# Three-by-three maxima stored by the first stage and used by all classes, in a second stage whose neighbouring tiles are of different classes

## What is computed

```python
x = x + _L0_conv_ref(_gn(x), L0_conv_W, L0_conv_bias)   # 1x1 product over 512 channels + 25 descriptors
x = x + _L1_conv_ref(_gn(x), w1, b1, w2, b2)
# layer 1, for each of the 16 x 512 planes:
s = relu(score)                        # one number a plane, from the plane means through two small products
q_s = clip(floor(s), 0, 5); q_b = q_s + 1
pools = [x, max over 3x3, 5x5, 7x7, 9x9, 11x11, 13x13]       # stride 1, same size
return frac_b * pools[q_b] + frac_s * pools[q_s] + x
```

## Time and profile before

| | us |
|---|---|
| median of 3 runs | 4183.77 (4174.26 to 4189.22) |
| the profiled execution | 4180.08 |
| its span in the trace | 4177.9 |
| PE busy | 3474.2 (83%) |
| DVE busy | 3378.0 (81%) |
| POOL busy | 2087.4 (50%) |
| ACT busy | 1981.8 (47%) |

### The profile page before, as it was taken

The page is one execution under the profiler, slowest core; times in us unless marked ns, Lnnn a source line. Parts: engine busy times, 40 slices in busy tenths (PEclk is TensorE's granted clock), DMA queues, the critical chain, the costliest instruction groups (busy, mean ns, idle before and its releaser), DMA issues. The chain is left out here.

```text
span 4177.9 us, 72982 instructions
## 1 busy us (share of the span) xinstructions
PE 3474.2 (83%) x22600; PEld 1981.8 (47%) x22601; DVE 3378.0 (81%) x3619; ACT 1981.8 (47%) x3227; POOL 2087.4 (50%) x1576
## 2 busy tenths in 40 slices
PE   4999999999999999999999996567678666666554
PEld 3666666666665666666666664223233222222221
DVE  5777777777777777777777766899989999999995
ACT  3545445445445545545445440664556544444342
POOL 3555555556555555555555541554444444454343
PEclk9999999999999999999999996878889888877777
DMA  5445445445454454455455233664478666565552
GB/s 195 154 156 185 164 157 187 158 164 181 161 175 168 165 176 166 162 177 178 147 177 187 98 128 74 258 244 186 184 293 339 269 254 244 232 247 197 222 199 81
DMA packets 252355, 782.10 MB, mean 187 GB/s; under 512 B 98150, under 2 KB 98150, under 8 KB 229990
## 3 DMA queue, kind: packets, MB, share of 16 engines
q1 hardware_dynamic: 219600, 417.85, 29.0%
q0 software_dynamic: 32288, 358.95, 21.9%
HBM read 428.22 MB, written 409.08 MB: 200 GB/s over the span
## 5 line engine op out<-in xcount | busy, mean ns | idle before, releaser
L1039 DVE TENSOR_TENSOR arena<-arena 128x2048 f32<-128x2048 f32 (+9 forms) x635 | 1454.8, 2319 | 66.4 <-issue 23.1
L439 POOL TENSOR_TENSOR arena<-arena 128x512 f16<-128x512 f32 x512 | 651.2, 1277 | 861.5 <-ACT arena L582 860.3
L1390 PE MATMUL psum<-arena 128*128 128x512 f32 x896 | 534.9, 682 | 461.5 <-issue 336.6
L448 POOL TENSOR_TENSOR arena<-arena 128x512 f32 (+1 forms) x512 | 639.7, 1271 | 293.6 <-ACT arena L594 288.2
L1219 PE MATMUL psum<-arena 128*128 128x512 f16 x2048 | 776.3, 379 | 1.0 <-ACT arena L594 1.0
L1221 PE MATMUL psum<-arena 128*128 128x512 f16 x2048 | 776.2, 379 | 0.0
L1220 PE MATMUL psum<-arena 128*128 128x512 f16 x2048 | 776.2, 379 | 0.0
L1196 PE MATMUL psum<-arena 128*128 128x256 f16 (+1 forms) x6344 | 712.7, 270 | 34.5 <-DVE arena L789 21.2
L580 ACT ACTIVATE arena<-arena,gbias,grstd 128x512 f32 (+1 forms) x512 | 413.7, 808 | 632.0 <-PE psum L1221 515.6
L1392 PE MATMUL psum<-arena 128*128 128x512 f32 x1072 | 604.5, 661 | 71.1 <-ACT psum L665 54.4
L679 ACT ACTIVATE arena<-psum 128x512 f32<-128x512 f32 x536 | 315.9, 598 | 716.4 <-PE psum L1392 704.4
(11 more groups left out here) (150 smaller groups left out, 3246.6 us busy)
## 6 DMA issues: line engine op xcount, KB each, us to landing
arena<-in_x SPq DMA_DIRECT2D x64, 2048.0 KB, 13.0
wide_planes<-arena SPq DMA_DIRECT2D x128, 1024.0 KB, 8.9
y_planes<-arena SPq DMA_DIRECT2D x64, 2048.0 KB, 7.7
arena<-arena SPq DMA_DIRECT2D x1536, 8.0 KB, 1.8
arena<-wide_planes,arena POOLq DMA_INDIRECT x72, 11.7
arena<-plane_records,arena POOLq DMA_INDIRECT x67, 7.8
arena<-y_planes,arena POOLq DMA_INDIRECT x67, 9.7
out<-arena POOLq DMA_INDIRECT x67, 9.2
```

The costliest lines, as they stand in the source:

```text
L439: pool.tensor_tensor(gl[:, ct, slot], g32[:, ct % 2, :], gh[:, ct, slot], ALU.subtract).then_inc(s_gl, 1)
L448: pool.tensor_tensor(y, y, relu[:, o % 2, :], ALU.add).then_inc(s_added, 1)
L1039: ins = dve.tensor_tensor(dst, a, b, ALU.max)
L1390: pe.matmul(dst, diag[:, s, 0, :], small[:, s, b * ROWS:(b + 1) * ROWS, 1:W + 1], start=False, stop=False, skip_group_check=True)
```

## The change

`wide_rows` now stores the maxima over 3 x 3 neighbours instead of those over 5 columns. It works on whole rows shifted by one against the chunk (`wide_span`: 7 rows for chunk 0, 8, and 9 for chunk 7), column direction first, in two groups of two channel tiles (four of one in chunk 7), and writes even columns to the left half of a row and odd ones to the right half. Its pair maxima lie in `wide` itself, so it waits for the last store ahead of its first operation; ScalarE's relu waits for all of it (`s_wide`) instead of its third operation.

In the second stage every class takes the stored planes as its source (now three buffers, `SRC`). Class 0 has no VectorE work left, its product reads the source; class 1 grows the bigger window from it and its smaller window's product reads it; classes 2 to 5 build their smaller window from it, in fewer elements. TensorE writes through a pattern that brings even and odd columns back together. And the numbering of tiles goes by columns of a table of 12 x 6: tile 6b + a has the place b + 12a in the order of class.

```diff
-        pairs_f = take(CT * ROWS * (W // 2 + 1))
-        pairs_m = pairs_f.rearrange("p (t h w) -> p t h w", t=CT, h=ROWS)
-        relu = pairs_f[:, 0:2 * CW].rearrange("p (s n) -> p s n", s=2)
-        wide_f = take(CT * CW)
-        wide = wide_f.rearrange("p (t h w) -> p t h w", t=CT, h=ROWS)
+        relu_f = take(2 * CW)
+        relu = relu_f.rearrange("p (s n) -> p s n", s=2)
+        wide_f = take(CT * (ROWS + 1) * W)
+        wide = wide_f.rearrange("p (t h w) -> p t h w", t=CT, w=W)
...
-        source = v(2 * (H + 2 * PADY) * W).rearrange("p (s h w) -> p s h w", s=2, w=W)
-        hbuf_f = v((H + 2 * PADR) * W)
-        hbuf = hbuf_f.rearrange("p (h w) -> p h w", w=W)
-        small_f = v(2 * H * (W + 2))
-        small = small_f.rearrange("p (s h w) -> p s h w", s=2, h=H)
-        big = v(2 * PIX).rearrange("p (s n) -> p s n", s=2)
-        half_m = v(36 * W)
+        source = v(SRC * PIX).rearrange("p (s h w) -> p s h w", s=SRC, w=W)
+        hbuf = v((H + 2) * W).rearrange("p (h w) -> p h w", w=W)
+        small = v(2 * PIX).rearrange("p (s h w) -> p s h w", s=2, w=W)
+        big = v(2 * PIX).rearrange("p (s h w) -> p s h w", s=2, w=W)
...
+        PAIR_OPS = 32
+        def wide_span(c):
+            return max(c * ROWS - 1, 0), H if c == CH - 1 else (c + 1) * ROWS - 1
...
                 sp.wait_ge(s_wide, i * CH + c + 1)
-                sp.dma_start(wide_v[bass.ds(i, 1), :, :, c * CW:(c + 1) * CW].rearrange("b p t n -> p (b t) n"),
-                             wide_f.rearrange("p (t n) -> p t n", t=CT)).then_inc(wide_stored, 16)
+                first, top = wide_span(c)
+                sp.dma_start(wide_v[bass.ds(i, 1), :, :, first * W:top * W].rearrange("b p t n -> p (b t) n"),
+                             wide_f.rearrange("p (t n) -> p t n", t=CT)[:, :, 0:(top - first) * W])\
+                  .then_inc(wide_stored, 16)
...
-                sp.wait_ge(s_wide, i * CH + 2 * q + 2)
+                sp.wait_ge(s_wide, i * CH + min(2 * q + 3, CH))
...
-            pool.iota(tnum_i, [[1, NT]], base=0, channel_multiplier=0).then_inc(s_iota, 1)
+            pool.iota(tnum_i.rearrange("p (b a) -> p b a", a=NCLS), [[1, NT // NCLS], [NT // NCLS, NCLS]], base=0,
+                      channel_multiplier=0).then_inc(s_iota, 1)
...
+            def gather_source(t):
+                if t >= SRC:
+                    pool.wait_ge(sourced[t % SRC], t // SRC * 16)
+                pool.indirect_dma_start(out=source[:, t % SRC, :, :].rearrange("p h w -> p (h w)"), out_offset=None,
+                                        in_=wide_dram[:, :],
                                         in_offset=bass.IndirectOffsetOnAxis(ap=src_ids[:, t:t + 1], axis=0),
-                                        bounds_check=NPL - 1, oob_is_err=False).then_inc(sourced[b % 2], 16)
+                                        bounds_check=NPL - 1, oob_is_err=False).then_inc(sourced[t % SRC], 16)
...
-                    act.wait_ge(s_middle, chunk)
+                    act.wait_ge(s_wide, chunk)
...
+                used = [0]
+                def op(dst, a, b, wait=True, signal=s_pairs):
+                    if wait and used[0]:
+                        dve.wait_ge(s_pairs, n * PAIR_OPS + used[0])
+                    dve.tensor_tensor(dst, a, b, ALU.max).then_inc(signal, 1)
+                    if signal is s_pairs:
+                        used[0] += 1
+                first, top = wide_span(c)
+                total = top - first
+                r = max(first, 1)
+                np_ = (min(top, H - 1) - r) // 2
                 dve.wait_ge(s_added, (n + 1) * CT)
-                dve.tensor_tensor(pairs_m[:, :, :, 1:half], y[:, :, :, 1:W - 2:2], y[:, :, :, 2:W - 1:2], ALU.max)\
-                    .then_inc(s_pairs, 1)
-                dve.tensor_tensor(pairs_m[:, :, :, 0:half + 1:half], y[:, :, :, 0:W:W - 1], y[:, :, :, 0:W:W - 1],
-                                  ALU.max).then_inc(s_pairs, 1)
-                dve.wait_ge(s_pairs, n * 4 + 2)
                 if not (isinstance(n, int) and n == 0):
                     dve.wait_ge(wide_stored, n * 16)
-                dve.tensor_tensor(wide[:, :, :, 0:W:2], pairs_m[:, :, :, 0:half], pairs_m[:, :, :, 1:half + 1],
-                                  ALU.max).then_inc(s_middle, 1)
-                dve.wait_ge(s_middle, n + 1)
-                dve.tensor_tensor(wide[:, :, :, 1:W - 2:2], wide[:, :, :, 0:W - 3:2], y[:, :, :, 3:W:2], ALU.max)\
-                    .then_inc(s_pairs, 1)
-                dve.tensor_tensor(wide[:, :, :, W - 1:W], wide[:, :, :, W - 2:W - 1], wide[:, :, :, W - 2:W - 1],
-                                  ALU.max).then_inc(s_pairs, 1)
-                dve.wait_ge(s_pairs, n * 4 + 4)
-                dve.tensor_tensor(wide[:, :, :, 2:W:2], wide[:, :, :, 2:W:2], y[:, :, :, 0:W - 3:2], ALU.max)\
-                    .then_inc(s_wide, 1)
+                step = 1 if total > ROWS else 2
+                for t in range(0, CT, step):
+                    ts = slice(t, t + step)
+                    pairs = wide[:, ts, 0:np_, :]
+                    column = relu_f[:, 0:step * total * W].rearrange("p (t h w) -> p t h w", t=step, w=W)
+                    inner = column[:, :, r - first:r - first + 2 * np_, :]
+                    op(pairs, y[:, ts, r:r + 2 * np_:2, :], y[:, ts, r + 1:r + 1 + 2 * np_:2, :])
+                    op(inner[:, :, 0::2, :], pairs, y[:, ts, r - 1:r - 1 + 2 * np_:2, :])
+                    op(inner[:, :, 1::2, :], pairs, y[:, ts, r + 2:r + 1 + 2 * np_:2, :], wait=False)
+                    if c == 0:
+                        op(column[:, :, 0:1, :], y[:, ts, 0:1, :], y[:, ts, 1:2, :], wait=False)
+                    if c == CH - 1:
+                        op(column[:, :, total - 1:total, :], y[:, ts, H - 2:H - 1, :], y[:, ts, H - 1:H, :], wait=False)
+                    even, odd = wide[:, ts, 0:total, 0:W // 2], wide[:, ts, 0:total, W // 2:W]
+                    op(odd, column[:, :, :, 0::2], column[:, :, :, 1::2])
+                    op(even[:, :, :, 0:1], odd[:, :, :, 0:1], odd[:, :, :, 0:1])
+                    op(even[:, :, :, 1:], odd[:, :, :, 1:], column[:, :, :, 1:W - 2:2], wait=False)
+                    done = t + step == CT
+                    op(odd[:, :, :, 0:W // 2 - 1], odd[:, :, :, 0:W // 2 - 1], column[:, :, :, 2::2],
+                       signal=s_wide if done else s_pairs)
+                assert used[0] <= PAIR_OPS
+                dve.sem_inc(s_pairs, PAIR_OPS - used[0])
...
-                link(dve.tensor_scalar(sel, tcls, 2.0, None, ALU.is_ge))
-                link(dve.scalar_tensor_tensor(sel, tcls, float(NCLS), sel, ALU.is_lt, ALU.mult))
+                link(dve.tensor_scalar(sel, tcls, float(NCLS), None, ALU.is_lt))
...
+                def split(a):
+                    return a.rearrange("p h (e j) -> p h e j", e=2)
+                def grown(src, dst, signal=s_own):
+                    even, odd = split(src)[:, :, 0, :], split(src)[:, :, 1, :]
+                    h_even, h_odd = split(inner)[:, :, 0, :], split(inner)[:, :, 1, :]
+                    op(h_even[:, :, 1:], odd[:, :, 0:31], odd[:, :, 1:])
+                    op(h_odd[:, :, 0:31], even[:, :, 0:31], even[:, :, 1:], wait=False)
+                    op(h_even[:, :, 0:1], odd[:, :, 0:1], odd[:, :, 0:1], wait=False)
+                    op(h_odd[:, :, 31:], even[:, :, 31:], even[:, :, 31:], wait=False)
+                    op(dst, hbuf[:, 0:H, :], hbuf[:, 2:H + 2, :], signal=signal)
...
+                if k == 2:
+                    grown(threes, sm_)
+                elif k == 3:
+                    m = split(bg)[:, :, 0, :]
+                    tw = lambda a: a.rearrange("p h (e j) -> p (h e) j", e=2)
+                    op(m[:, :, 1:31], odd[:, :, 0:30], even[:, :, 2:])
+                    op(tw(inner)[:, :, 0:32:31], tw(threes)[:, :, 0:31:30], tw(threes)[:, :, 1:32:30], wait=False)
+                    op(h_even[:, :, 1:31], m[:, :, 1:31], even[:, :, 0:30])
+                    op(h_odd[:, :, 1:31], m[:, :, 1:31], odd[:, :, 2:], wait=False)
+                    m = bg[:, 1:31, :]
+                    two = lambda a: a.rearrange("p (a b) w -> p a b w", b=2)
+                    op(m, inner[:, 1:60:2, :], inner[:, 4:63:2, :])
+                    op(two(sm_)[:, 0:32:31, :, :], two(inner)[:, 0:32:31, :, :], two(inner)[:, 1:31:29, :, :], wait=False)
+                    op(sm_[:, 2:61:2, :], m, inner[:, 0:59:2, :])
+                    op(sm_[:, 3:62:2, :], m, inner[:, 5:64:2, :], wait=False)
...
+                grown(threes if k == 1 else sm_, bg, signal=s_pool)
...
+                        if not (isinstance(t, int) and t == 0):
+                            dve.wait_ge(s_pool, t)
...
+                        if lo in (0, NCLS):
...
+                            if not (isinstance(t, int) and t < 2):
+                                dve.wait_ge(s_mix, (t - 1) * 8)
+                            dve.wait_ge(sourced[u % SRC], wide_loaded)
...
```

(13 more changed lines are left out.)

170 lines of the change are left out of this document (57 added, 113 removed).

## The result

| | before | after |
|---|---|---|
| median of 4 runs, us | 4185.63 (4174.26 to 4189.22) | 4679.69 (4679.1 to 4681.43) |
| span of the profiled execution, us | 4177.9 | 4677.3 |
| last aggregation of y's statistics (L889 before, L910 after), end of the first stage | 2553.2 | 3127.7 |
| from there to the end of the span | 1624.7 | 1549.6 |

The ratio is 1.1186, with a 95% interval of 1.1164 to 1.1208: 494 us slower. The first stage became 574.5 us longer, the rest 75.1 shorter. Forecast were +500 and -105.

A forecast was written before the change was run, and what follows sets the result against it. TensorE was taken to bound the first stage and VectorE the second; after the change VectorE's loop would bound the first. 4180.1 + 500 (stage one) - 105 (stage two) = 4575, 4579 on the median, forecast 4580, range 4300 to 4740.

The forecast's parts named there:

- The likeliest case: First stage: VectorE's loop with POOL's collisions sets a 22.9 us chunk, +500 us; total 4580, chance 0.57.
- Rival 1: First stage: VectorE is the bound but POOL hardly collides, period 20.7 to 21.5; total about 4340, chance 0.20.
- Rival 2: First stage: new maxima fit into VectorE's idle 4.7 us, chunk stays at TensorE's 19.0; total 4075, chance 0.13.
- Rival 3: First stage: the single buffer's store lands late and binds; total 4750 to 4940, chance 0.10.
- the signs named: Trace marks of being right: image near 183 us, VectorE over 90%, TensorE near 80%, mask waits each chunk, 18 us stalls.
- The base of 19.0 a chunk: First stage before the change: TensorE-bound image of 151.8 us over 8 chunks, 19.0 us each.
- `wide_rows` without collisions: First stage, VectorE: the new maxima take 10.7 us a chunk in the mean, against 6.0 before.
- Collisions: First stage: POOL's low parts beside `wide_rows` cost VectorE 2.6 us a chunk, 0.4 + 3 x 0.75.
- All else: First stage: VectorE's loop around `wide_rows`, 8.7 us, plus 0.9 a chunk for what an image has once.
- in the case that VectorE is never early: First stage: assumption for counting VectorE's loop from the first mask, giving a period of 8.7 us plus `wide_rows`.
- the same slack covers it: First stage: a falling TensorE clock is hidden by some 4 us of idle time in each chunk.
- The eleven turns: Second stage: each pass through classes 0 to 5 stalls VectorE 18 + 6.5 = 24.5 us, in sum 270.

The follow-up runs named there:

- after_tiny_low: The changed kernel with POOL's low parts cut to 16 of 512 columns: 4406.99 us (ratio 1.0556).
- s1_only: The changed kernel's new first stage with the second stage of the kernel before: 4742.74 us (ratio 1.1354).
- before_mixed: The kernel before with only the new mixed numbering of tiles: 4248.59 us (ratio 1.0159).
- before_mixed11: The kernel before with its first 66 tiles mixed in six cycles of eleven, the last six, five of them empty, left at the end: 4196.05 us (1.0035).
- after_warm: The changed kernel with eight added, unused TensorE products of 384 columns ahead of the Gram products that wait for a mask: 4618.5 us (1.1055).
- after_late_sorted: The changed kernel with statistics of x moved behind the second y statistic and tiles in order of class: 4530.12 us (1.0837).
- after_sorted: The changed kernel with its tiles in order of class again: 4629.8 us (ratio 1.1072).

## Why the prediction came out right, and where its terms were off

**The sign and half of the mechanism held.** The likeliest case, VectorE's loop with collisions, gave 4580; it is 4680, within its own range of 4480 to 4700. That `wide_rows` and its collisions make the first stage longer is shown; that VectorE would be the engine that never waits is not so. Rival 1 (hardly any collisions) is refuted by after_tiny_low: only without them does the kernel come to 4407, and rival 1 had 4340. Rival 2 (all fits into idle time) is refuted by s1_only, +564. Rival 3 (the store binds) is refuted by the store's 4.7 us and the lack of any wait for it before the last `wide_rows`. Of the signs named, low parts inside a `wide_rows` of 12 to 14 us, TensorE near 80% (84) and class 1 tiles with 18 us of idle ahead are there. Three are not: the image is 194.6 us and not near 183, VectorE is busy 80% there and not over 90%, and TensorE waits for a mask in five of eight chunks and not in each.

**Part of the closeness is luck.** `wide_rows` with its collisions was put at 13.3 and is 12.2; what lies around it was put at 9.6 and is 12.05. With the first number and the base of 19.4 right and the second as it stood, the sum would have been 4180 + 128 x (9.6 + 12.23 - 19.4) - 105 = 4386, nearer rival 1's 4340 than the time measured.

**Stage one, forecast +500, measured +574.5.** Term by term:

- The base of 19.0 a chunk was 19.4. The stretch of the earlier trace rows was taken for an image and was 3.3 us short of one. Alone this would have made the forecast 50 us lower.
- `wide_rows` without collisions was put at 10.7 and is 9.72. The waits in it were priced at 0.22 each; only the first of a group costs that. A group of six operations with three more waits takes 3.56 us, and the formula without waits has 3.59: the starts and ends in the trace leave 0.03 us at each of the three, and the two operations that don't wait overlap the one before by 0.08.
- Collisions, forecast 2.6, measured 2.51. Per low part 0.72 and 0.8 against the forecast's 0.75. The Trainium skill (SBUF — State Buffer, section Who interferes with whom) has VectorE operations with two SBUF inputs and POOL operations that read SBUF exclude each other for the whole instruction. The trace agrees in kind; by that rule a low part was to cost 0.94, and the runs show less.
- All else was put at 8.7 + 0.9 = 9.6 and is 24.28 - 12.23 = 12.05. This is the step that failed: "in the case that VectorE is never early" and, for the clock, "the same slack covers it". From the first mask to `wide_rows` it was to be 6.35 in each chunk; in the table above it is 6.8 to 11.1, 9.2 in the mean: 2.8 more, where all that stands between the end of one `wide_rows` and the next first mask came out 0.4 shorter than counted. VectorE is early in most chunks: its masks wait for TensorE (1.20 in the row at 1556.71), its reciprocal for ScalarE (1.56 at 1575.05, as in three of eight chunks). From 500 to 2700 us, 90 chunks, VectorE waits 127.7 us for TensorE, 81.7 for POOL and 57.4 for ScalarE, 2.9 a chunk. Part of TensorE's work runs at its lower clock, as the row of 0.50 shows; the slack was in TensorE's busy share, but not at the products that VectorE waits for.

So the period of a middle image is 22.9 - 1.0 - 0.1 + 2.45 = 24.3, and over the base of 19.4 it is 4.9 where 3.9 was forecast. Over the fifteen images from the first to the last statistics of y the mean is (3127.7 - 244.4) / 15 = 192.2, since the last two are shorter (for the last two no statistics of x are left to make); before it is (2553.2 - 227.8) / 15 = 155.0. 15 x 37.2 = 558 and 16.6 of the first image make the 574.5.

**Stage two, forecast -105, measured -75.** From first to last maxima it is 1434.5 us, 22 above the forecast 1412. VectorE's work was put at 1142 us and is 1119.5, right to 2%. The eleven turns were put at 24.5 each, 18 for products and 6.5 for the source. Eight of them have 144.4 us for products and 59.7 for the source, 18.1 and 7.5 each. The other three, 34.25, 26.56 and 34.50, all behind a cycle that ends in an empty tile, wait for the source alone, 31.8 in the mean. In sum 299.4 in place of 270, and some 15 of short waits were not counted. The first maxima came 80.7 us behind the first stage (3208.4 against 3127.7), where before had 64.8 (2618 against 2553.2): 16 in place of the 5 put down. The end is 34 us behind the last maxima (4677.3 against 4643) and was 49 before (4177.9 against 4129): -15 where -10 stood. That the empty tiles no longer stand at the end was counted as that gain alone; before_mixed and before_mixed11 show, in the old list of operations, that amid the others they cost 53. The forecast took the mixed order as the frame of its sum and never priced the sorted one, which wins 125 us where the mixed one wins 75. One bound was also added up wrong: with every gather in time the stage would have been 11 x 6.5 = 71.5 us below the forecast, some -176 and not -165.

What stays open: how the loop comes to its pattern of long and short chunks, over how many chunks it closes, and how the 2.45 us divide between the slow clock, the waits through ScalarE and POOL, and relu's wait for all of `wide_rows`. after_warm took 0.37 a chunk off this part, net of what its added products cost, and 0.44 off the collisions.

## What to carry to other kernels

Price a move of work onto an engine "with idle time" by the loop that the engine stands in, not by its busy share: count from the last operation of the moved work through each engine that waits for the next, and over several rounds (here the eight chunks of an image), since waits that come in some rounds alone don't show in one. When two terms of such a sum are checked only by their total, a right total can hide two wrong terms. When work is added ahead of a wait of TensorE, the products behind the wait have to be priced at the lower clock as well. Where VectorE's operations on two inputs in SBUF stood beside POOL's low parts, each low part cost 0.7 to 0.8 us, so they are better laid apart; and empty tiles, which cost 53 us amid the others, belong at the end of an order with a fixed run-ahead.

## What the runs showed of the hardware

- An operation of VectorE on 128x512 took 690 ns in after_tiny_low, and 915 in the mean with POOL's whole low parts; these took 1.27 us singly inside a `wide_rows` in place of 1.16: both engines lose.
- A wait between two operations of VectorE cost 0.21 after the first operation of a group and 0.03 at each of the three further on. With the waits covered and half the size, fourteen operations took 4.59 us, 0.79 less than their sum of 5.38 by the formula, and seven of full size 4.45.
- 24 Gram products took 2.79 us with no wait ahead and a granted clock of 1.00, and 4.02 behind a wait of 6.25 with a granted clock of 0.50, the lower of the two levels (1.2 and 2.4 GHz). Eight products that compute nothing of use, ahead of them, won 61 us, in part by moving the low parts out of `wide_rows`' way.
- Gathers and scatters of whole planes moved 420 GB/s over 161 us with the DMA engines full, in after_sorted; the highest slice of the kernel before has 339.
- The two halves of the change, and the two edits of after_late_sorted, added up within 2 us.
